# Last feed-forward of a four-layer vision tower: output stored by group of tiles in two sets of rows, norms in groups of 4, 4, 2 and 1 tiles, and gate and up products that begin at the first eight tiles

## The reference

```python
    def _L3_ffn_ref(x, clip_x, clip_down, w_gate, w_up, w_down):
        QMAX = 127.0
        def _act_fake_quant(x, clip_factor):
            scale = jax.nn.sigmoid(clip_factor) * jnp.max(jnp.abs(x)) / QMAX
            return jnp.clip(_ste_round(x / scale), -QMAX - 1.0, QMAX) * scale
        def _weight_fake_quant(w):
            scale = jnp.max(jnp.abs(w), axis=1, keepdims=True) / QMAX
            return jnp.clip(_ste_round(w / scale), -QMAX - 1.0, QMAX) * scale
        xq = _act_fake_quant(x, clip_x[0])
        gate = jnp.einsum('bsh,ih->bsi', xq, _weight_fake_quant(w_gate))
        up = jnp.einsum('bsh,ih->bsi', xq, _weight_fake_quant(w_up))
        h = _act_fake_quant(jax.nn.silu(gate) * up, clip_down[0])
        return jnp.einsum('bsi,hi->bsh', h, _weight_fake_quant(w_down))
    ...
    h = _layernorm(h + _L3_ffn_ref(h, L3_ffn_clip_x, L3_ffn_clip_down, L3_ffn_w_gate, L3_ffn_w_up, L3_ffn_w_down), axis=-1)
    return h
```

## Time and profile before

| | |
|---|---|
| time, three runs, median | 1123.51 us (1122.18 to 4631.71) |
| time of the profiled execution | 1126.98 us |
| its span, first to last instruction | 1125.2 us |
| PE busy | 926.1 us (82%) |
| DVE busy | 605.5 us (54%) |
| ScalarE busy | 525.5 us (47%) |
| POOL busy | 329.4 us (29%) |
| transfers over the span | 47.40 MB, mean 42 GB/s |
| granted clock of TensorE, mean | 0.874 of full speed |

### The profile page before, as it was taken

One profiled execution on the slowest core, in us unless ns is written; L12 is line 12 of the kernel. 1 busy time (PEld: TensorE's weight loads), 2 busy tenths in 40 slices (PEclk: granted clock), 3 DMA queues, 4 the chain that ended last, 5 costly groups with the idle time before them and its releaser, 6 DMA issues. The chain is left out here.

```text
span 1125.2 us, 26130 instructions
## 1 busy us (share of the span) xinstructions
PE 926.1 (82%) x10336; PEld 684.7 (61%) x10336; DVE 605.5 (54%) x1301; ACT 525.5 (47%) x940; POOL 329.4 (29%) x419
## 2 busy tenths in 40 slices
PE   4889958389999799768995499999479999988664
PEld 4878735267777557557884244445367778777332
DVE  3566746556666379745663433323554554532385
ACT  2354638376656289635441255552123333522354
POOL 0202320545543100030331334441453544531101
PEclk9999968699999889879996699999589999966685
DMA  5300020200000100001004952224200000000001
GB/s 182 113 3 2 3 108 11 80 1 2 1 0 1 43 3 1 0 11 39 3 3 138 404 164 40 47 38 99 82 2 3 2 3 3 3 2 2 1 1 43
DMA packets 24466, 47.40 MB, mean 42 GB/s; under 512 B 4664, under 2 KB 16115, under 8 KB 23714
## 3 DMA queue, kind: packets, MB, share of 16 engines
q1 hardware_dynamic: 19524, 39.09, 10.0%
q0 software_dynamic: 3936, 5.51, 3.0%
q10 hardware_dynamic: 894, 1.23, 0.3%
HBM read 38.35 MB, written 7.47 MB: 41 GB/s over the span
## 5 line engine op out<-in xcount | busy, mean ns | idle before, releaser
L2719 PE MATMUL psum<-L2f_EW,weights_even 128*64 x176 | 81.6, 607 | 1.8 <-ACT weights_even L2418 1.3
L2720 PE MATMUL psum<-L2f_W,weights_even 128*64 128x512 f32 x176 | 81.6, 607 | 0.0
L2379 POOL DMA_INDIRECT expert_sums<-weights_even,L2f_target x20 | 35.0, 1750 | 77.5 <-DVE weights_even L2601 54.1
L1048 PE MATMUL psum<-L_cT,weights_odd 128*128 128x222 f32 (+1 forms) x192 | 49.4, 392 | 9.4 <-DVE L_by_sin L937 8.3
L2614 DVE TENSOR_TENSOR weights_even<-psum,weights_even 128x512 f32<-128x512 f32 x22 | 15.2, 692 | 73.4 <-PE psum L2720 71.3
L2235 PE MATMUL psum<-weights_even,L1f_H 128*111 128x256 f32 x176 | 47.4, 428 | 7.4 <-DVE L1f_H L2166 7.4
L937 DVE TENSOR_TENSOR L_by_cos<-psum,vectors_odd 128x444 f32<-128x444 f32 (+1 forms) x48 | 26.6, 554 | 49.9 <-PE psum L1048 49.4
L2426 ACT ACTIVATE L2f_W<-L2f_EW 128x1024 f32 x44 | 46.3, 1053 | 13.7 <-DMA L2f_EW<-experts 7.5
L876 ACT ACTIVATE L_PT<-psum 101x296 f32<-101x296 f32 x32 | 13.3, 416 | 83.7 <-PE psum L1089 83.1
L2719 PEld LDWEIGHTS psum<-L2f_EW,weights_even 128*64 128x64 f32 x176 | 22.7, 139 | 44.5 <-issue 44.5
L419 ACT ACTIVATE L_PT<-psum 101x296 f32<-101x296 f32 x64 | 26.9, 421 | 48.2 <-PE psum L615 48.1
(11 more groups left out here) (452 smaller groups left out, 2665.2 us busy)
## 6 DMA issues: line engine op xcount, KB each, us to landing
L2f_EW<-experts SPq DMA_DIRECT2D x24, 512.0 KB, 13.0
weights_even<-L_w SPq DMA_DIRECT2D x4, 1024.0 KB
patch_ring<-patches SPq DMA_DIRECT2D x11, 333.0 KB, 5.1
expert_sums<-L_blank SPq DMA_DIRECT2D x1, 1184.0 KB
out<-X SPq DMA_DIRECT2D x10, 111.0 KB
weights_odd<-L_wo SPq DMA_DIRECT2D x1, 1024.0 KB
expert_rows<-X SPq DMA_DIRECT2D x1, 960.0 KB
expert_sums<-X SPq DMA_DIRECT2D x1, 960.0 KB
```

Of the source, the lines that this page charges most:

```text
L1048: mm = nc.tensor.matmul(bank[:, h * NC2:h * NC2 + width(u)], wu[:, (2 * g + h) * 128:(2 * g + h + 1) * 128], cT[:, u % 2, n // 4, 0:width( ...
L2379: nc.gpsimd.indirect_dma_start(sums[:, :], bass.IndirectOffsetOnAxis(ap=target[:, j:j + 1], axis=0), Y[:, j % 2, :], None, compute_op=ALU. ...
L2719: nc.tensor.matmul(core.bank(bank)[PAIR[0], :], xsT[:, j % 2, c, PAIR[0]], own, start=c == 0, stop=c == KD - 1)
L2720: mm = nc.tensor.matmul(core.bank(bank)[PAIR[1], :], xsT[:, j % 2, c, PAIR[1]], cols(W1[:, part], KD, NF)[:, c], start=c == 0, stop=c == K ...
```

## The change

There are three edits, all in `quantised_glu`.

- The norms go by `ENDS = [(0, 4), (4, 4), (8, 2), (10, 1)]`. ScalarE applies those of the first three groups (tiles 0 to 9), DVE that of tile 10 alone.
- SP waits for a group, not a tile, and stores a group in two transfers: rows 0 to 95 of its tiles, then rows 96 to 110. The last tile goes as 64 rows and 10 rows. Eight transfers take the place of eleven.
- PE waits for four of ScalarE's six copies before step 0 of the gate and up products, and for all six before step 1.

```diff
-        tail = SplitNorm(core, st, sb)
+        ENDS = [(0, 4), (4, 4), (8, 2), (10, 1)]
+        ON_ACT = 3
+        tail = SplitNorm(core, st, sb, ENDS)
...
             @block.sync
             def _(sp):
-                for t in range(NT):
-                    if t < GROUPS[2][0]:
-                        sp.wait_ge(tail.act_norm, t + 1)
-                    else:
-                        sp.wait_ge(tail.dve_norm, t - GROUPS[2][0] + 1)
-                    if t < NT - 1:
-                        sp.dma_start(out[t * R:(t + 1) * R, :], X[:R, t, :]).then_inc(stored, 16)
-                    else:
-                        skip = NT * PER - B
-                        sp.dma_start(out[t * R:, :], X[skip * T:R, t, :]).then_inc(stored, 16)
-                sp.wait_ge(stored, 16 * NT)
+                skip = (NT * PER - B) * T
+                for t0, k in ENDS[:ON_ACT]:
+                    sp.wait_ge(tail.act_norm, t0 + k)
+                    by_row = out[t0 * R:(t0 + k) * R, :].rearrange("(t p) d -> p t d", p=R)
+                    for rows in (slice(0, 96), slice(96, R)):
+                        sp.dma_start(by_row[rows], X[rows, t0:t0 + k, :]).then_inc(stored, 16)
+                sp.wait_ge(tail.dve_norm, 1)
+                for rows in (slice(skip, skip + 64), slice(skip + 64, R)):
+                    sp.dma_start(out[(NT - 1) * R + rows.start - skip:(NT - 1) * R + rows.stop - skip, :], X[rows, NT - 1, :]).then_inc(stored, 16)
+                sp.wait_ge(stored, 16 * 2 * len(ENDS))
 
             @block.gpsimd
             def _(pool):
-                for g in range(len(GROUPS)):
+                for g in range(len(ENDS)):
                     tail.on_pool(pool, g)
...
-                    for g, (t0, k) in enumerate(GROUPS):
+                    for g, (t0, k) in enumerate(ENDS):
                         if t == t0 + k - 1:
                             tail.stats(g)
...
-                tail.on_dve(dve, 2)
+                tail.on_dve(dve, 3)
...
                 tail.on_act(act, 1)
+                tail.on_act(act, 2)
...
-                pe.wait_ge(xt_done, NXB)
                 for n, (g, c) in enumerate(steps):
+                    if n < 2:
+                        pe.wait_ge(xt_done, 4 if n == 0 else NXB)
                     after(pe, h_done, n - 1)
```

## The result

| | before | after |
|---|---|---|
| median, 20 runs each | 1123.91 us (1119.73 to 4631.71) | 1118.82 us (1112.08 to 1126.77) |
| ratio after to before | | 0.9936, 95% interval 0.9919 to 0.9953 |
| profiled execution: time | 1126.98 us | 1122.27 us |
| its span | 1125.2 us | 1120.4 us |
| start of the stage's first maximum | 1053.40 | 1056.57 |

The ratio says 0.64% less, 7.2 us of 1123.9 (5.3 to 9.1); 7.8 were forecast. It counts as no change by the 2% bound, and the interval lies clear of 1. The two medians are 5.1 us apart, a quotient of 0.9955, just outside that interval. The measured median, 1118.82, is 3.1 us above the 1115.7 of the forecast and 0.3 above the upper end of its range, 1118.5; the ratio, laid on the 1123.51 from which the forecast started, gives 1116.3, inside the range.

The account below looks back on a forecast made before the run. The output stores' queue on three DMA engines, not arithmetic, was taken to set the end. 7.2 us there plus 0.6 from the earlier start, 7.8 off the median 1123.51, gave 1115.7 us, range 1112.5 to 1118.5.

Parts of the forecast that it names:

- the 2% bound: Whole kernel: a measurement tells about 2% from no change, 22 us; chance of "same" 0.98.
- Three engines set the end, and the change takes them off the path: Output stores: 111-row stores use three DMA engines at 72 GB/s; new ones reach 250 GB/s, span ends 7.2 us earlier.
- The last norm: DVE's norm of tile 10, regrouped: ends at 1114.9 instead of 1115.29, 0.4 us earlier.
- From the last issue to the release: SP's end: 10-row store issued 1115.35 to 1115.7, SP released at 1117.0, between bounds 1116.55 and 1118.0.
- The lower bound: SP's release after the 10-row store: at least 1.2 us from its issue at 1115.35, 1116.55.
- The upper bound: SP's release after the 10-row store: 2.3 us, from a 30 KB load, after 1115.7, 1118.0.
- The earlier start: Gate and up products: PE starts step 0 0.69 us earlier, of which 0.6 us passes down the chain.
- a rise that stays in its place: PE's clock in steps 0 and 1: if its rise keeps its time, only 0.35 of the 0.69 us is gained.
- Rival 1: PE's steps 0 and 1: clock rises much earlier, gaining 2.2 us in place of 0.6, time 1114.1; chance 0.10.
- the missing hole: PE ahead of step 0: its 0.69 us wait for ScalarE's sixth copy disappears, so the clock might rise earlier.
- The sum: Whole kernel: 7.2 us from the end plus 0.6 from the earlier start, 7.8 us in all.

Follow-up runs that it names:

- e_stores: Kernel before with the store edit alone; tail (start of DVE's last maximum over H to end of span) 32.91 us against 38.92, ratio to before 0.997.
- e_111: Changed kernel with each group stored by one transfer of 111 rows and the last tile by one of 74; tail 41.16 us.
- e_97: Changed kernel with the groups' stores split as 97 and 14 rows in place of 96 and 15; tail 64.64 us.
- e_two: Changed kernel with ScalarE issuing the 15 rows of tiles 8 and 9 and the last tile's 10 rows; tail 31.85 us, ratio to before 0.9903.
- e_start: Kernel before with PE's early start alone; front (stage's first maximum to start of DVE's last) 31.97 us against 32.88, tail 38.90.
- e_again: The changed kernel once more, unaltered; front 31.04 us, tail 32.17 us, ratio to before 0.9903.
- both filled holes: Changed kernel with PE waiting for all six copies before step 0 and doing two unused products meanwhile, profiled twice; fronts 33.51 and 33.03 us.
- e_late: Changed kernel with PE waiting for all six copies before step 0, as before; front 33.12 us, tail 32.08 us.
- e_104: Changed kernel with the groups' stores split as 104 and 7 rows; tail 32.11 us.

## Why the prediction was right, and where it was off

*Three engines set the end, and the change takes them off the path.* Right, and shown: e_stores takes 6.0 us off the tail, e_111 without the split adds 2.2, and e_97 with one engine is 33 us longer than with 96 rows. The tail lost 7.11 where 7.2 was forecast. The rule in the Trainium skill against splitting a transfer in two (page "DMA: Bandwidth & Descriptors", section "Rules for kernel authors") did not hold for 111 rows, as the rows had said.

*The last norm.* Forecast 0.4 earlier; 0.45 measured (29.01 to 28.56), and 0.4 between the mean of the ten profiles with the new groups (28.74) and that of the four with the old (29.14). The steps can be followed: two tiles of statistics 0.75 and 0.25, one tile 0.43 and 0.18, POOL's power of one 0.55. One was off: from the end of DVE's share for tiles 8 and 9 (1113.59) to ScalarE's start at 1115.36 it was 1.8 us, not the 1.4 forecast; POOL's power of the two alone took 0.98. So SP was issuing for them until 1117.29, and the last pair began at 1117.34, 0.2 behind the norm.

*From the last issue to the release.* The last pair's issue began 28.75 into the tail; the forecast had it at 28.7, and the release at 30.7. It was 30.9. The 10-row store began 0.67 us behind the 64-row one: the forecast had quoted a row with 0.77 between the two of a pair, and yet put it 0.4 behind. From the 10-row store's issue to the release it was 1.5 us (1118.01 to 1119.51), between the bounds of 1.2 and 2.65 and close to the 1.65 that the forecast took. The lower bound was short in the time to the last byte, not behind it (windows of the changed kernel):

```profile
1119.10:1119.20 0.10, 0.50 0.06 10
1119.20:1119.50 0.30, 0.50 0.00 0
```

The last data go out before 1119.2, 1.1 to 1.2 us after that issue began where 0.9 was forecast, and 0.3 more to the release is what was forecast. The upper bound, the 2.3 us of a load of 30 KB, was counted from the end of the issue and lay 1.1 too high. What decides, as e_two shows, is the 64-row store, 2.1 to 2.2 us from its issue to the release. The Trainium skill's fixed cost of about 2.0 us for a transfer (page "DMA: Bandwidth & Descriptors", section "Anatomy of one DMA", fitted on transfers that GpSimd issues) agrees with that.

*The earlier start.* The direction was right and the size too small. Forecast 0.69 for PE and 0.6 for the chain. PE's step 0 began 9.29 into the front before and 8.39 after, 0.90 earlier: I had added the transposes' busy time up to its modelled end, but the first product starts before that end (1063.92, while the transposes' row ends at 1064.12 in e_start). Then the fronts: seven of the old start average 33.20, seven of the new 31.75, **1.45 us less**. This is the term that was mis-sized. Of it, 0.9 is the start itself, in full: H0 is 13.50 or 13.51 in all seven of the old and never above 12.63 in the new, and fronts of like clock differ by 0.9 (31.97 to 32.01 against 32.88 with no fall; 32.37, of e_two, against a mean of 33.26 with one). The forecast had taken something off the 0.69, for a rise that stays in its place. The rest is the clock. In three of seven new executions (after, e_97, e_again) it rose between 10.0 and 10.6, in none of the old before 12.4. Rival 1, given 0.10, thus came true in part of the executions, with its 2.1 us at DVE's step 1 (15.85 before, 13.72 after) against the 2.2 worked out. In the changed kernel's profile most of this was lost again in the steps of 333 columns:

```profile
1067.00:1068.00 1.00, 1.00 (x7) 0.93 0.00 0
...
1080.00:1081.00 1.00, 0.74 (x4) 0.90 0.00 0
1081.00:1082.00 1.00, 0.51 (x2) 0.50 0.00 0
...
1083.00:1084.00 1.00, 1.00 (x6) 0.50 0.08 16
1084.00:1085.00 1.00, 1.00 (x7) 0.90 0.00 0
```

These are the changed kernel's windows of PE (length, busy, clock). The clock is up from 1067.1, goes down just before 1081, and is back at 1084.2. PE's products of 333 columns then take twice as long and DVE waits for them, 0.80 us at one step. Without such a fall the fronts of the new start are 31.97 to 32.01 (three, clock up at 13.1) and 30.88 and 31.04 (up at 10.0 and 10.3); with it they are 32.02 and 32.37. Only two of the seven new executions had a fall, and six of the seven old; with so few I do not lay that on the start. That the pair's own front came out at 0.86, near the 0.6 of the forecast, is partly luck, since in the changed kernel's profile the early rise and the fall nearly cancel. For the early rise there is one like pair: in the kernel before the clock fell 0.37 us behind the front's start, in the changed kernel 0.33 behind it, and it rose at 14.0 and at 10.6. That speaks for the new start as its cause, in one pair. Whether the missing hole or the earlier step 0 brings it is open, since both filled holes met the other kind of execution.

*The sum.* 7.8 was forecast; the profiles say 7.97 for this pair and 7.1 + 1.45 = 8.6 on average over fronts (8.2 with the tail of e_again); the two ratios say 7.2 (5.3 to 9.1) and, in the later set of runs, 10.9 (6.8 to 15.0). Why the stage begins up to 11 us earlier or later from execution to execution I did not look into.

## What to carry to other kernels

Look at the share of DMA engines, not only at GB/s: a share of 0.20 with nothing else going on means three engines of 16, and the number of rows in a transfer decides it. Cut 111 rows into 96 and 15 where such a store stands on the path (loads were not tried here), and check that both parts have a divisor near 16; one row in the wrong part costs more than all other edits here gained. Speed up what stands ahead of a queue (the norms) only after the queue itself, since before that it is worth nothing.

## What the runs showed of the hardware that was not expected

- A queue that is full of one engine's work holds the issuing engine: 12.54, 16.46 and 8.05 us for a store of 14 rows behind one of 97, 3.26 us for the one of 74 rows behind groups of 111, against 0.3 to 0.6 us for one when the queue is short (0.63 and 0.31 in e_two).
- The 64-row store takes 2.1 to 2.2 us from its issue to the release of the engine that waits (after, e_stores, e_late, e_again, e_two; 2.4 in e_104), and issuing the 10 rows beside it from another engine leaves that as it is.
- The granted clock fell to 0.50 for about three microseconds in the middle of the products of 333 columns in eight of fourteen profiles, beginning 24 to 27 us into the front. In the 3 us before the fall PE was busy for 1.0 to 1.5 us; in the kernel before it was busy for 1.1 of 3.0 us (1077.4 to 1080.4), and the clock stayed at 1.00. Among kernels of the same start a front with such a fall is 0.15 to 1.1 us longer.
